# Plane differences of the normalised data: vector engine and PSUM, or pool engine and SBUF

## The reference

```python
x = x + 0.5 * ffn(layernorm(x))
x = x + attention(layernorm(x))     # conv of width 3, 1024 -> 768, then causal attention in blocks of 128, projection
x = x + 0.5 * ffn(layernorm(x))

def ffn(x):                          # 8 experts only scale the channels
    routing = softmax(x @ gate_w.T)
    out = (x * (routing @ in_channel_scale)) @ sign(weight).T
    return out * (routing @ out_channel_scale) + bias
```

## Time and profile before

| Engine | busy us | share of the span |
|---|---|---|
| PE | 916.2 | 90% |
| DVE | 715.1 | 70% |
| ACT | 419.6 | 41% |
| POOL | 360.4 | 35% |

### The profile page before, as it was taken

The page is one execution under the profiler, slowest core; times in us unless marked ns, Lnnn a source line. Parts: engine busy times, 40 slices in busy tenths (PEclk is TensorE's granted clock), DMA queues, the critical chain, the costliest instruction groups (busy, mean ns, idle before and its releaser), DMA issues.

```text
span 1018.1 us, 15266 instructions
## 1 busy us (share of the span) xinstructions
PE 916.2 (90%) x4992; PEld 697.7 (69%) x4992; DVE 715.1 (70%) x1491; ACT 419.6 (41%) x1127; POOL 360.4 (35%) x305
## 2 busy tenths in 40 slices
PE   4788989898899999999988998998899798999997
PEld 2466667675433677788766786777677576887885
DVE  5677777679998898655586488189458857667552
ACT  3533333221134326243675356256435544433331
POOL 2144444546653221000233133133133432554565
PEclk9999999999999999999999999999999999999999
DMA  9432332333224341684003032212153485333432
GB/s 289 157 125 88 122 117 89 116 112 105 92 94 132 131 146 68 227 290 173 14 11 93 2 83 85 62 41 72 52 136 84 143 256 159 125 125 146 133 115 104
DMA packets 43012, 119.97 MB, mean 118 GB/s; under 512 B 7232, under 2 KB 16448, under 8 KB 41536
## 3 DMA queue, kind: packets, MB, share of 16 engines
q1 hardware_dynamic: 42944, 119.11, 35.8%
HBM read 87.64 MB, written 31.46 MB: 117 GB/s over the span
## 4 chain that ended last, share of the span: by engine, by line
PE 61%; DVE 21%; issue 7%; ACT 6%; DMA 3%; POOL 2%; SPq 0%; POOLq 0%; DVEq 0%; ACTq 0%
PE a_p_g L1846 17%; PE a_p_g L634 11%; PE f_p_m L634 6%; PE c_p_m L1292 4%; PE c_p_m L1294 3%; PE c_p_m L1296 3%; PE c_p_m L1295 3%; PE a_p_s L1870 2%; PE a_p_o L1894 2%; ACT a_s L1642 2%; DVE a_sums L1746 2%; PE a_p_s L577 1%; DVE f_nst L399 1%; DVE a_s L1743 1%; DVE a_pt L1760 1%
## 5 line engine op out<-in xcount | busy, mean ns | idle before, releaser
L1575 POOL TENSOR_TENSOR a_s<-a_s,a_sums 128x512 f32<-128x512 f32 x64 | 66.6, 1040 | 279.6 <-DVE a_sums L1752 279.6
L280 POOL TENSOR_TENSOR f_y<-f_y,f_res 128x512 f32<-128x512 f32 x64 | 84.3, 1317 | 143.7 <-DVE f_y L492 143.0
L1642 ACT ACTIVATE a_s<-a_s,a_nmx 128x128 f32<-128x128 f32 x256 | 99.3, 390 | 41.1 <-DVE a_nmx L1748 41.1
L634 PE MATMUL f_p_m<-f_wsign,f_a_hi 128*128 128x512 f32 x256 | 106.4, 416 | 0.0
L1846 PE MATMUL a_p_g<-c_xs_hi,x_room 128*128 128x512 f32 x256 | 94.6, 417 | 10.1 <-DVE c_xs_lo L1708 9.5
L634 PE MATMUL f_p_m<-f_wsign,f_a_lo 128*128 128x512 f32 x256 | 102.5, 400 | 0.0
L634 PE MATMUL a_p_g<-f_wsign,f_a_hi 128*128 128x512 f32 x256 | 102.5, 400 | 0.0
L634 PE MATMUL a_p_g<-f_wsign,f_a_lo 128*128 128x512 f32 x256 | 100.4, 392 | 0.0
L277 POOL TENSOR_TENSOR f_res<-f_res,f_hbias 128x512 f32<-128x512 f32 x64 | 84.2, 1316 | 8.7 <-DMA f_res<-x_after_attention 6.2
L1292 PE MATMUL c_p_m<-c_vf,c_ring_f 128*128 128x512 f32 (+1 forms) x192 | 73.9, 542 | 7.0 <-DVE c_ring_f L964 6.9
L1294 PE MATMUL c_p_m<-c_vh,c_ring 128*128 128x512 f32 x192 | 75.4, 393 | 5.2 <-issue 2.9
(11 more groups left out here) (222 smaller groups left out, 2200.8 us busy)
## 6 DMA issues: line engine op xcount, KB each, us to landing
c_raw<-in_conv_w_dram SPq DMA_DIRECT2D x24, 768.0 KB, 4.3
f_w_raw<-in_w_t_dram SPq DMA_DIRECT2D x8, 1024.0 KB, 11.0
f_res<-in_x_dram SPq DMA_DIRECT2D x16, 512.0 KB, 4.3
x_after_ffn<-f_y SPq DMA_DIRECT2D x8, 1024.0 KB, 6.4
f_xin<-x_after_attention SPq DMA_DIRECT2D x8, 1024.0 KB, 5.0
f_res<-x_after_attention SPq DMA_DIRECT2D x16, 512.0 KB, 4.3
out_dram<-f_y SPq DMA_DIRECT2D x8, 1024.0 KB, 6.3
f_xin<-in_x_dram SPq DMA_DIRECT2D x7, 1024.0 KB, 5.0
```

Of the source, the lines that this page charges most:

```text
L280: pool.tensor_tensor(y[:, p, t, h], y[:, p, t, h], res[:, t, h], ALU.add).then_inc(y_done, 1)
L634: last = pe.matmul(p_m[:, q % 2, :], part[p][:, k, q // 2 * P:q // 2 * P + P], wsign[:, k, q % 2 * HALF:q % 2 * HALF + HALF], start=(k == ...
L1575: pool.tensor_tensor(s[:, r], s[:, r], sums[:, r].unsqueeze(2).broadcast_to([P, 4, P]), ALU.mult).then_inc(probs_ready, 1)
L1642: done = act.activation(s[:, r, h, :], s[:, r, h, :], ACT.Exp, bias=nmx[:, r, h:h + 1], scale=SCALE, accum_out=sums[:, r, h:h + 1])
```

## The change

The differences of groups 0 to 5 move from DVE to POOL. ACT now copies all four planes of a chunk (128x512) to SBUF, PE waits for that copy alone (`n_copied`), and POOL subtracts in place in SBUF, two instructions of 128x8x64 for a whole group, in the pass two later (`differences(g - 2)`), between its first residual addition and its first y addition. A new semaphore `differenced` counts them. Groups 6 and 7 keep DVE's differences out of PSUM with two banks in turn; chunk 0 of group 6 still waits for the copy. Three orders change besides:

- POOL: the power for the output (L273, now L293) goes from the start of the pass to behind the first residual addition and the differences.
- SP: the first residual tile of a group is asked for as soon as two quarters of the group before are added, ahead of the load of x and no longer behind it.
- DVE: the statistics of group g+4 are one piece again; in the last pass the differences of group 6, the statistics of group 7's first tile and the first filters stand in another order, and `last_normalise(0)` stands behind the last eviction and not in front of it.

The diff, without unchanged surroundings:

```diff
     def body(g, p):                                   # sync
+            if exists(g - 1):
+                sp.wait_ge(y_done, 4 * g - 2)
+                load_res(g, 0)
             if X is not None and late(g):
                 sp.wait_ge(t_full, 4 * NG)
                 conv.load(sp, 0)
...
             if exists(g - 1):
-                for t in range(FT):
-                    sp.wait_ge(y_done, 4 * g - 2 + 2 * t)
-                    load_res(g, t)
+                sp.wait_ge(y_done, 4 * g)
+                load_res(g, 1)
                 store(g - 1, 1 - p)
...
+        def differences(g):                            # pool
+
+            quads = bass.ds(g * (FTOK // 4) + 1, FTOK // 4)
+            pool.wait_ge(n_copied, 4 * g + 5)
+            for to, of in ((2, 0), (3, 1)):
+                last = pool.tensor_tensor(Xp[:, :, to, quads], Xp[:, :, to, quads], Xp[:, :, of, quads], ALU.subtract)
+            last.then_inc(differenced, 1)
+
         def body(g, p):
...
             if exists(g + 3):
                 power(g + 3)
-            if X is not None and exists(g - 1):
-                pool.wait_ge(n_var, g)
-                pool.tensor_tensor(nrstd[:], nvpe[:], minus_half[:], ALU.pow).then_inc(n_rstd, 1)
             for q in range(4):
...
                 pool.tensor_tensor(res[:, t, h], res[:, t, h], hbias[:, h], ALU.add).then_inc(res_biased, 1)
+                if q == 0 and X is not None and exists(g - 2):
+                    differences(g - 2)
+                if q == 0 and X is not None and exists(g - 1):
+                    pool.wait_ge(n_var, g)
+                    pool.tensor_tensor(nrstd[:], nvpe[:], minus_half[:], ALU.pow).then_inc(n_rstd, 1)
                 pool.wait_ge(res_biased, 4 * g + q + 1)
...
                 if q == 1 and X is not None and late(g):   # vector
-                    dve.wait_ge(n_differenced, 4 * (NG - 2))
+                    dve.wait_ge(differenced, NG - 2)
                     conv.early_data(dve, Xp, 0)
...
             act.wait_ge(n_full, 4 * g + c + 2)             # scalar, copy_normed
-            act.copy(plane_part(g, c, slice(0, 2)), normed_planes(g, c)[:, :, 0:2, :]).then_inc(n_copied, 1)
+            planes = slice(0, 2) if by_two(g) else slice(0, 4)
+            act.copy(plane_part(g, c, planes), normed_planes(g, c)[:, :, planes, :]).then_inc(n_copied, 1)
...
             pe.wait_ge(y_normed, g + 2 + (late(g) and c // 2))   # tensor, normed
-            two = isinstance(g, int) and (g == NG - 1 or g == NG - 2 and c > 0)
-            wait(pe, n_differenced, 4 * g + c - two)
-            if two:
+            if by_two(g) and (g, c) != (NG - 2, 0):
                 pe.wait_ge(t_copied, 4 * NG)
+                wait(pe, n_differenced, 4 * (g - NG + 2) + c - 1)
+            else:
+                wait(pe, n_copied, 4 * g + c + 1)
```

## The result

| | before | changed |
|---|---|---|
| median of the timed runs | 1020.89 us (5 runs, 1016.97 to 1022.78) | 1012.55 us (5 runs, 1010.17 to 1016.28) |
| profiled execution; span | 1019.92; 1018.1 us | 1013.02; 1011.2 us |
| PE, DVE busy | 916.2, 715.1 us | 915.5, 704.2 us |
| ACT, POOL busy | 419.6, 360.4 us | 425.0, 375.2 us |

The ratio is 0.9925 (95% interval 0.9898 to 0.9952); the forecast was 1011.7. In two later series it was 0.9924 (0.9897 to 0.9950) and 0.9913 (0.9892 to 0.9934). All three intervals lie wholly under 1, so the change is faster, by about 0.8%; that it is by more than the half per cent of the forecast, the third interval shows and the first leaves just open. The kernel before took 1020.89 us here and not the 1018.08 of the forecast: the difference of the medians is -8.3 us, where -6.4 was forecast.

A forecast was written before the change was run, and what follows sets the result against it. Bound: a loop between PE and DVE in the first stage's passes, neither full. Terms -2.85 - 2.3 + 1.5 - 0.2 - 2.6 = -6.45 took the timed median from 1018.08 to 1011.7 us; 8-of-10 range 1007.5 to 1017.0.

The forecast's parts named there:

- case A: The forecast itself for the whole kernel: terms summing to -6.45 us, timed median 1011.7 us; chance 0.50.
- Differences off DVE: Passes 1 to 3: PE waits for ACT's copy alone and DVE's eviction comes 0.95 us earlier; -2.85 us in all.
- What POOL's differences cost: Passes 2 to 4: L408 waits 0.3 us for POOL, plus 0.2 for the power running into the normalisation; +1.5 us.
- Passes 4 to 6: Passes 4 and 5 hold counted as nothing; pass 6 hold +0.9, removed waits in 5 and 6 twice -0.55; together -0.2 us.
- Early load: Passes 1 to 4: residual tile asked for earlier, so POOL's addition stops slowing the normalisation in 1, 3 and 4; -2.3 us.
- The last pass: Pass 7: output normalisation ends about 1.0 us later, but DVE's new order then pays; -2.6 us taken, range 1.5 to 3.3.
- My walk of the list: Pass 7: DVE's new order stepped through with old lengths, second tile's statistics at 241.15 instead of 243.94, 2.8 us earlier.
- B: Rival: L408 on DVE is not held up by POOL, which returns 2.7 us: 1009.0 us; chance 0.20.
- C: Rival: PE's longer waits for low parts make its clock fall in three further passes, +5.1 us: 1016.8 us; chance 0.22.
- D: Rival: POOL's strided subtraction takes 3.1 us, sum +8.8 us, 1026.9 us; 8.4 us per us of the difference; chance 0.08.

The follow-up runs named there:

- u3: Changed kernel with the differences of groups 0 to 5 back on DVE; early load, moved power and new pass 7 order kept: 1014.13 us, ratio 0.9952 to before.
- w2: Changed kernel with POOL's differences of groups 3 and 4 behind the first y addition of passes 5 and 6, group 5 in quarter 3 of pass 6: 1012.18 us.
- w3: As w2, but with the differences of group 3 back at the start of pass 5: 1010.09 us, ratio 0.9916 to before.
- b1: Kernel before with the early request of the first residual tile alone: 1019.52 us, ratio 0.9984 to before.
- u1: Changed kernel with the first residual tile asked for late, behind the load of x, as before: 1017.62 us, ratio 0.9976 to before.
- u2: Changed kernel with the old order of pass 7 alone: 1014.62 us, ratio 0.9930 to before.
- v1: Changed kernel with POOL's differences of groups 0 to 5 by tiles in quarter 3 of the pass before: 1011.67 us, ratio 0.9922 to before.
- d1: Changed kernel with four POOL subtractions for a group instead of two: 1023.36 us, ratio 1.0030 to before.
- a0: The changed kernel unaltered, in a second series: 1011.07 us, ratio 0.9924 to before.
- a1: The changed kernel unaltered, in a third series beside w3: 1011.41 us, ratio 0.9913 to before.

## Why the prediction was right, term by term

The forecast was case A, -6.45 us. The terms as measured, from the profiles of before, u3 and changed:

| term | predicted | measured |
|---|---|---|
| differences on POOL, passes 1 to 6 (changed against u3) | -2.85 + 1.5 - 0.2 = -1.55 | -2.69 |
| early load, with the moved power (u3 against before, passes 1 to 4) | -2.3 | -2.40 |
| last pass (changed against before) | -2.6 | -2.45 |
| sum up to the planes | -6.45 | -7.5 |

**Differences off DVE.** Pass 1 has no POOL differences and isolates the term: 25.45 to 24.54, -0.91 against -0.95. PE's waits moved as said: in pass 2 the one at chunk 3 is gone, and the one at the second low part grew, though from 0.29 to 0.52 only and not by 0.5.

**What POOL's differences cost.** The mechanism is right and the size was more than twice too large. L424 was to take 0.5 in passes 2 to 4 and over 1 in the later ones; it takes 0.34 and 0.91 to 0.94. I had added the instruction's own 0.17 to the hold of 0.3, but the hold contains it: L424 begins at 95.27 and ends with POOL's subtraction. The price is 0.17. The other 0.2, the power beside the normalisation, is 0.02 (1.55 against 1.53). By passes 2 and 3 (0.72 and 0.70 gained where pass 1 gains 0.91) it is 0.2 a pass, not 0.5. Over three passes that is 0.9 of the 1.1 us by which this term was too small.

**Passes 4 to 6.** I had given 24.7 for pass 4 and counted the removed waits as nothing; it is 23.84. The faster normalisation gave 0.70, the differences another 0.27 net of POOL's hold (I had nothing for them, with a bound of 0.4, and 0.5 for the hold). In passes 5 and 6 two errors cancel: the hold costs 0.4 in pass 6 (24.43 against 24.04 to 24.06 in w2 and w3) and not 0.9, but the removed waits gave some 0.2 there and 0.3 in pass 5 and not 0.55 each. Why the hold of 0.74 costs only 0.4 is not shown; PE's wait for the low part did grow by 0.74, from 2.11 to 2.85.

**Early load.** -2.40 as predicted, but my working credited the load alone. b1 shows that the load without the moved power brings nothing, and u1 that its lack costs the changed kernel 6.8 us in passes 1 to 3. In pass 4 u1 loses nothing (23.85), so there the gain is the power's alone. The moved power alone, without the early load and with DVE's differences, was not run. Pass 2, where I expected no gain, gave 0.06.

**The last pass.** -2.45 is right as a sum, and in part by luck: the order gives 2.0 (u2, up to the six data instructions), the hold of L424 takes 0.7 (u3, v1, w3), and the other 1.2 are left for the moved power, which I had not named: I gave the new order all of the gain. That last size is a difference of the others, and no run has it alone. My walk of the list ended well, with the second tile's statistics at +21.1 (241.15 - 220.03) against +21.47, but its steps were off by more and cancelled: 0.6 us for the tile's normalisation, which took 1.75 beside POOL as before, 1.6 for the two data instructions, which took 2.89, and 1.2 us between them for which no row stands.

**Rivals.** B fell with L424's 0.34 and 0.94. By the rule of the Trainium skill in "SBUF — State Buffer", section "Who interferes with whom", DVE in a two-port mode and GpSimd lock each other out for a whole instruction; the trace agrees, for the strided 128x2 too, with its 0.34 and 0.94. C did not come by PE's 0.52 us waits: passes 1 to 5 keep the full clock in all three profiled executions of the changed kernel. It is real, though, in u1 and d1, at waits of 2.5 and 2.6 us. In pass 6 PE's wait grew from 2.11:

```profile
194.33 0.39 PE L626 MATMUL c_p_m<-f_rT,f_ics 128*128 128x256 f32 x1 [2.85 <-DVE f_a_lo L407]
```

The lower clock did not last longer on average for that. The six profiled executions with a wait of 2.85 us (changed, a0, a1, u1, u2, d1) had 3.4, 0, 6.8, 3.4, 3.4 and 0 us of it in pass 6; the six with 2.11 to 2.48 (before, b1, u3, w2, w3, v1) had 3.4 each. D fell with 1.28 us a subtraction. Its slope of 8.4 us for each us, 10.8 for the doubling, came out near 12.9, but half of it stood on L408, which kept its 0.34: in d1 the normalisation paid 2.1 a pass, as D had it, and the clock 4.5 in all, which D had not. The nearness of the numbers is luck.

**The total.** The profiled execution gives -6.9 and not -7.5, since 1.3 came at the start and 1.9 went in the rest, both about as much as they vary between executions of the changed kernel. The medians differ by 8.3, 8.0 and 9.4 us in the three series. The 7.5 us of the passes are a ratio of 0.9927, which lies inside all three intervals, so no remainder is shown. That the median came within 0.9 us of the forecast is partly luck: the kernel before was 2.8 us above the time that I started from, and the change gave 1.9 more.

## What to carry to other kernels

When work moves from DVE to POOL, count not its length but which DVE instructions begin while it runs: instructions with a PSUM operand passed unharmed here, two large ones in SBUF alone lost 2.1 us, and a tiny one was held until POOL's ended. A wait that goes from one engine's list can come back at another place of it, as DVE's 13.7 us did; only the pacing loop counts. A cheap-looking early load pays only if the engine that uses it is not parked at another semaphore. And judge a 1 us change by the lengths of the passes it touches, not by the total.

## What was not expected of the hardware

- Instructions of 128x16 in SBUF (0.17 us alone) took 0.64 to 0.80 and 1.22 us beside POOL (u1, w2), and one of 128x2 took 1.16 (u1): the smallest instructions pay the largest factor, 7 here.
- The large statistics (128x512 in SBUF, 0.62 us each) kept their length beside POOL's additions and subtractions (2.46 to 2.48 for four in every pass looked at).
- POOL loses too: its subtractions took 2.98 for two beside held DVE work (u1) and 3.00 in d1, against 2.56, and a filter sum of 1.3 us alone took 5.19 beside six DVE instructions in every kernel but u2.
- The same program had 0, 3.4 and 6.8 us of the lower clock in the same pass in three executions: 22.87, 24.43 and 25.69 us.
